# Down LoRA between token groups: expert weights transposed to the layout of the LoRA rows, in place of LoRA rows transposed to token order

## The reference

```python
gate = x @ W_gate + _lora(x, sA_gate, sB_gate, scale) + _expert_lora(x, A_gate, B_gate, w, scale)
up = x @ W_up + _lora(x, sA_up, sB_up, scale) + _expert_lora(x, A_up, B_up, w, scale)
hidden = jax.nn.silu(gate) * up
out = hidden @ W_down + _lora(hidden, sA_down, sB_down, scale) + _expert_lora(hidden, A_down, B_down, w, scale)
# _expert_lora: xA = einsum('bld,edr->bler', x, A); (einsum('bler,erd->bled', xA, Bm) * scale * w).sum(axis=2)
```

## Time and profile before

| | us |
|---|---|
| three executions | 732.37, 734.18, 735.18 |
| median | 734.18 |
| span of the profiled execution, first to last instruction | 731.8 |
| TensorE busy in it | 715.5 |
| VectorE busy | 376.6 |
| ScalarE busy | 262.3 |
| start of the attention's first denominators | 171.9 |
| first border between groups (last down projection to next first down) | 383.6 to 402.1 |
| last down projection's last matmul starts | 720.6 |

### The profile page before, as it was taken

How to read it: one execution, slowest core, us unless ns; L and a number is a source line. 1 busy time by engine, 2 the same in 40 slices (tenths; PEclk the granted TensorE clock), 3 DMA queues, 4 the chain that set the end, 5 groups by cost and what they waited for, 6 DMA issues and landing times.

```text
span 731.8 us, 10129 instructions
## 1 busy us (share of the span) xinstructions
PE 715.5 (98%) x3356; PEld 574.9 (79%) x3356; DVE 376.6 (51%) x715; ACT 262.3 (36%) x409; POOL 123.6 (17%) x293
## 2 busy tenths in 40 slices
PE   7999999998999999999999999999999999999997
PEld 5888888875776767888878888888788888788886
DVE  5666556676666665444425444325543335534433
ACT  4343333563431432333324333324333325333222
POOL 3544555420632641000000000000000000000000
PEclk9999999999999999999999999999999999999999
DMA  7766555326555645000010500010500001300001
GB/s 244 273 201 199 184 187 202 115 116 241 232 182 203 226 149 197 34 0 0 0 57 25 206 0 0 0 27 30 229 0 0 0 2 56 115 0 0 0 0 59
DMA packets 22754, 72.99 MB, mean 100 GB/s; under 512 B 2560, under 2 KB 2816, under 8 KB 20688
## 3 DMA queue, kind: packets, MB, share of 16 engines
q1 hardware_dynamic: 22560, 72.46, 27.8%
q0 software_dynamic: 176, 0.30, 0.2%
HBM read 51.78 MB, written 20.97 MB: 99 GB/s over the span
## 4 chain that ended last, share of the span: by engine, by line
PE 88%; DVE 5%; issue 2%; POOL 2%; ACT 1%; DMA 1%; DVEq 0%; SPq 0%; POOLq 0%
PE bank L1115 18%; PE bank L1116 18%; PE bank L1117 18%; PE bank L1326 17%; PE bank L1301 5%; PE bank L1313 4%; PE bank L1226 2%; PE bank L1142 1%; PE bank L1352 1%; PE bank L1178 1%; DMA w_raw<-in_wkT 1%; PE bank L1150 1%; PE bank L1132 1%; PE bank L1234 1%; PE bank L1345 1%
## 5 line engine op out<-in xcount | busy, mean ns | idle before, releaser
L1115 PE MATMUL bank<-x,up_h 128*128 (+1 forms) x352 | 138.1, 392 | 2.1 <-DVE qf L985 1.2
L1116 PE MATMUL bank<-x,up_h 128*128 (+1 forms) x352 | 137.3, 390 | 0.0
L1117 PE MATMUL bank<-x,up_l 128*128 (+1 forms) x352 | 137.0, 389 | 0.0
L1055 DVE TENSOR_TENSOR hf<-bank,silu 128x512 f32<-128x512 f32 x44 | 30.4, 691 | 157.2 <-issue 137.5
L1115 PEld LDWEIGHTS bank<-x,up_h 128*128 128x128 f32 x352 | 66.1, 188 | 19.0 <-issue 2.1
L594 ACT ACTIVATE hid_h<-hf 128x512 fp32r<-128x512 f32 x44 | 27.8, 632 | 146.3 <-DVE hf L1055 146.3
L1117 PEld LDWEIGHTS bank<-x,up_l 128*128 128x128 f32 x352 | 66.1, 188 | 14.1
L1116 PEld LDWEIGHTS bank<-x,up_h 128*128 128x128 f32 x352 | 66.1, 188 | 13.8
L799 DVE TENSOR_TENSOR up_l<-up_raw,up_h 128x1024 fp32r<-128x1024 f32 x45 | 55.6, 1236 | 37.1 <-ACT up_h L594 37.0
L1326 PE MATMUL bank<-dn_h,hid_h 128*128 128x512 f32 x176 | 69.8, 396 | 0.0
L1326 PE MATMUL bank<-dn_h,hid_l 128*128 128x512 f32 x176 | 69.2, 393 | 0.0
(11 more groups left out here) (169 smaller groups left out, 1260.3 us busy)
## 6 DMA issues: line engine op xcount, KB each, us to landing
x<-scr_x SPq DMA_DIRECT2D x8, 2048.0 KB, 7.6
up_raw<-in_ffn_up SPq DMA_DIRECT2D x11, 768.0 KB, 5.2
scr_x<-xt SPq DMA_DIRECT2D x16, 512.0 KB, 4.8
xin<-in_x SPq DMA_DIRECT2D x16, 256.0 KB, 5.8
scr_z<-zt SPq DMA_DIRECT2D x16, 256.0 KB, 2.2
x3r<-in_x SPq DMA_DIRECT2D x16, 256.0 KB, 3.5
scr_att<-x3r SPq DMA_DIRECT2D x16, 256.0 KB, 2.1
z<-scr_z SPq DMA_DIRECT2D x4, 1024.0 KB, 5.0
```

The source lines that it names most:

```text
L1055: nc.vector.tensor_tensor(hf[:], ps_u[:], silu[:], ALU.mult).then_inc(h_done, 1)
L1115: nc.tensor.matmul(dst, lh, rh, start=start, stop=False, **kw)
L1116: nc.tensor.matmul(dst, lh, rl, start=False, stop=False, **kw)
L1117: return nc.tensor.matmul(dst, ll, rh, start=False, stop=stop, **kw)
```

## The change

The rows of `ps_zd` are no longer turned. Instead the expert weights are: at the start of each group VectorE spreads `wtok` of the group to `wcur` (`weights_of`: each weight eight times, and 1/8 in the columns behind for the shared LoRA), TensorE transposes its four tiles into `ps_t` (`weights_transposed`, behind the second chunk's up projection), and ScalarE copies them to `wexp` (`weights_out`). At the end of the group one multiply on VectorE gives the weighted rows, `zw` = `ps_zd` x `wexp` (`lora_down_weighted`). ScalarE rounds them twice (`zd1`, `zd2`), VectorE subtracts for the low parts (`lora_down_lo`), and the two tiles are used as the weights of `lora_add`, which moves one gate projection earlier, to just behind the up projection of the next group's first chunk. The shared columns of `A_down` are computed twice (80 rows in `ps_zd` instead of 72), since the low part of the shared rows is kept beside the high one. In the tail the transposes and the filler of 9 go; the filler of 6 stays. For `bdn`, VectorE's two subtractions become one over rows 0 to 95, and ScalarE rounds the eight shared rows once more and signals `bdn_done`, behind `queries(0, (2, 3))`.

```diff
@@ -42,7 +42,8 @@
...
 UPC = UPW + UPB
-DNC = D + ER + R
+DNR = ER + 2 * R
+DNC = D + DNR
 SH = ER
...
@@ -200,11 +201,11 @@
...
         res = at("res", [P, GT, D])
-        zdc = at("zdc", [ER + R, GN])
-        zdf = at("zdf", [P, GT, ER])
-        zds = at("zds", [P, GT, R])
-        zdst = at("zdst", [P, GT, 2, P], F32R)
-        zdt = at("zdt", [P, 2, GT, P], F32R)
+        wcur = at("wcur", [P, GT, P])
+        wexp = at("wexp", [P, GN])
+        zw = at("zw", [P, GN])
+        zd1 = at("zd1", [P, GN], F32R)
+        zd2 = at("zd2", [P, GN], F32R)
...
@@ -712,6 +713,8 @@
...
             queries(0, (2, 3))
+            act.wait_ge(bdnl_done, 1)
+            round_to(bdn[SH:SH + R, 1], bdn_raw[SH:SH + R, 1]).then_inc(bdn_done, 1)
             lora_out(TILES - 1)
...
@@ -736,6 +739,8 @@
...
                     split_up(c + 1, 1 - s, n)
+                if before is not None:
+                    lora_down_hi(before)
                 if not start:
...
@@ -744,36 +749,25 @@
...
                     split_dn(c, s, 0)
-                if before is not None:
-                    stack_hi(before)
                 act.wait_ge(h_done, n + 2)
...
-            def lora_copy(g):
-
-                act.wait_ge(zd_ready, g + 1)
-                round_to(zdc[:], ps_zd[0:ER + R, :]).then_inc(zdc_done, 1)
-
-            def stack_hi(g):
-                act.wait_ge(zdf_done, g + 1)
-                round_to(zdst[:, :, :, 0:ER], zdf[:].unsqueeze(2).to_broadcast([P, GT, 2, ER]))
-                round_to(shared_cols(zdst), zds[:].unsqueeze(2).to_broadcast([P, GT, 2, R])).then_inc(zdh_done, 1)
-
-            def stack_out(g):
-                act.wait_ge(zdt_ready, g + 1)
-                round_to(zdt[:, 0].rearrange("p k n -> p (k n)"), ps_t[:])
-                round_to(zdt[:, 1].rearrange("p k n -> p (k n)"), ps_zd[:]).then_inc(zdt_done, 1)
+            def lora_down_hi(g):
+                act.wait_ge(zw_done, g + 1)
+                round_to(zd1[0:ER, :], zw[0:ER, :])
+                round_to(zd2[0:DNR, :], zw[0:DNR, :]).then_inc(zdh_done, 1)
+
+            def weights_out(g):
+                act.wait_ge(wexp_ready, g + 1)
+                round_to(wexp[:], ps_t[:]).then_inc(wexp_done, 1)
...
                 n = g * FC
-                if before is not None:
-                    lora_copy(before)
                 chunk(n, 0, 0, first=True, before=before)
-                if before is not None:
-                    stack_out(before)
                 chunk(n + 1, 1, 1)
+                weights_out(g)
                 with act.Fori(0, (FC - 3) // 2) as i:
...
@@ -787,9 +781,7 @@
...
                 group(g, before=g - 1)
-            lora_copy(GROUPS - 1)
-            stack_hi(GROUPS - 1)
-            stack_out(GROUPS - 1)
+            lora_down_hi(GROUPS - 1)
...
@@ -1012,9 +1004,7 @@
...
             dve.wait_ge(bdnh_done, 1)
-            for r0, r1 in ((0, ER), (SH2, P)):
-                last = sub(bdn[r0:r1, 1], bdn_raw[r0:r1, 1], bdn[r0:r1, 1])
-            last.then_inc(bdn_done, 1)
+            sub(bdn[0:SH2, 1], bdn_raw[0:SH2, 1], bdn[0:SH2, 1]).then_inc(bdnl_done, 1)
             queries(0, (2, 3))
...
@@ -1059,18 +1049,20 @@
...
-            def lora_rows(g):
-
-                dve.wait_ge(zdr_ready, g + 1)
-                zd = ps_t[:, 0:GT * (ER + R)].rearrange("p (j n) -> p j n", j=GT)
-                nc.vector.tensor_scalar(zds[:], zd[:, :, ER:], RSCALE, None, ALU.mult)
-                nc.vector.tensor_tensor(zdf[:].rearrange("p j (e r) -> p j e r", e=E),
-                                        zd[:, :, 0:ER].rearrange("p j (e r) -> p j e r", e=E),
-                                        wtok[:, bass.ds(g * GT, GT), :].unsqueeze(3).to_broadcast([P, GT, E, R]),
-                                        ALU.mult).then_inc(zdf_done, 1)
-                dve.wait_ge(zdf_done, g + 1)
+            def weights_of(g):
+                nc.vector.tensor_copy(wcur[:, :, 0:ER].rearrange("p j (e r) -> p j e r", e=E),
+                                      wtok[:, bass.ds(g * GT, GT), :].unsqueeze(3).to_broadcast([P, GT, E, R])
+                                      ).then_inc(wcur_done, 1)
+
+            def lora_down_weighted(g):
+                dve.wait_ge(zd_ready, g + 1)
+                dve.wait_ge(wexp_done, g + 1)
+                nc.vector.tensor_tensor(zw[0:DNR, :], ps_zd[0:DNR, :], wexp[0:DNR, :], ALU.mult).then_inc(zw_done, 1)
+
+            def lora_down_lo(g):
                 dve.wait_ge(zdh_done, g + 1)
-                stack_lo(zdst, zdf, zds).then_inc(zdst_done, 1)
+                sub(zd1[ER:2 * ER, :], zw[0:ER, :], zd1[0:ER, :])
+                sub(zd2[SH2:SH2 + R, :], zw[SH:SH + R, :], zd2[SH:SH + R, :]).then_inc(zdl_done, 1)
...
@@ -1081,12 +1073,16 @@
...
                 n = g * FC
-                chunk(n, 0, 0, due=None if before is None else lambda: lora_rows(before))
+                if before is not None:
+                    lora_down_weighted(before)
+                chunk(n, 0, 0, due=None if before is None else lambda: lora_down_lo(before))
                 if before is None:
...
                     dve.wait_ge(att_out, 16 * TILES)
-                    nc.vector.memset(zdst[:].bitcast(F32), 0.0).then_inc(late_clear, 1)
+                    nc.vector.memset(wcur[:, :, ER:], RSCALE)
+                    nc.vector.memset(zd2[:].bitcast(F32), 0.0).then_inc(late_clear, 1)
                     dve.wait_ge(late_clear, 1)
+                weights_of(g)
                 chunk(n + 1, 1, 1, due=None if before is None else lambda: results(before))
...
@@ -1103,7 +1099,8 @@
...
                 late_group(g, before=g - 1)
-            lora_rows(GROUPS - 1)
+            lora_down_weighted(GROUPS - 1)
+            lora_down_lo(GROUPS - 1)
             results(GROUPS - 1)
...
@@ -1310,7 +1307,7 @@
...
                     for i, (h, w) in enumerate(((hid_h, dn_h), (hid_h, dn_l), (hid_l, dn_h))):
-                        d = nc.tensor.matmul(ps_zd[0:ER + R, :], w[:, s, D:], h[:, s, :], start=(first and i == 0),
+                        d = nc.tensor.matmul(ps_zd[0:DNR, :], w[:, s, D:], h[:, s, :], start=(first and i == 0),
                                              stop=(last and i == 2), skip_group_check=True)
...
@@ -1329,29 +1326,20 @@
...
-            def lora_rows(g):
-
-                pe.wait_ge(zdc_done, g + 1)
+            def weights_transposed(g):
+                pe.wait_ge(wcur_done, g + 1)
                 for j in range(GT):
-                    last = nc.tensor.transpose(ps_t[:, j * (ER + R):(j + 1) * (ER + R)], zdc[:, j * P:(j + 1) * P],
-                                               ident[0:ER + R, 0:ER + R])
-                last.then_inc(zdr_ready, 1)
-
-            def lora_stack(g):
-
-                pe.wait_ge(zdst_done, g + 1)
-                for b, dst in enumerate((ps_t, ps_zd)):
-                    for j in range(GT):
-                        last = nc.tensor.transpose(dst[:, j * P:(j + 1) * P], zdst[:, j, b, :].bitcast(F32), ident[:])
-                last.then_inc(zdt_ready, 1)
+                    last = nc.tensor.transpose(ps_t[:, j * P:(j + 1) * P], wcur[:, j, :], ident[:])
+                last.then_inc(wexp_ready, 1)
             def lora_add(g):
-                pe.wait_ge(zdt_done, g + 1)
+                pe.wait_ge(zdl_done, g + 1)
                 for j in range(GT):
-                    for b in range(2):
-                        last = nc.tensor.matmul(ps_out[j][:], zdt[:, b, j, :], bdn[:, b, :], start=False, stop=(b == 1),
-                                                skip_group_check=True)
-                    last.then_inc(o_ready, 1)
+                    cols = slice(j * P, (j + 1) * P)
+                    nc.tensor.matmul(ps_out[j][:], zd1[:, cols], bdn[:, 0, :], start=False, stop=False,
+                                     skip_group_check=True)
+                    nc.tensor.matmul(ps_out[j][:], zd2[:, cols], bdn[:, 1, :], start=False, stop=True,
+                                     skip_group_check=True).then_inc(o_ready, 1)
...
@@ -1364,14 +1352,11 @@
...
                     gate_or_up(g, n, 0, 0, first=True)
-                    lora_rows(before)
                     gate_or_up(g, n, 0, 1)
-                if before is not None:
-                    lora_stack(before)
+                    lora_add(before)
                 gate_or_up(g, n + 1, 1, 0)
-                if before is not None:
-                    lora_add(before)
                 gate_or_up(g, n + 1, 1, 1)
+                weights_transposed(g)
                 down(g, n, 0, first=True)
...
@@ -1386,9 +1371,6 @@
...
                 group(g, before=g - 1)
-            lora_rows(GROUPS - 1)
-            keep_busy(ps_g, 9)
-            lora_stack(GROUPS - 1)
             keep_busy(ps_g, 6)
...
@@ -1432,7 +1414,7 @@
...
         ffn_up[:, :, UPW + a * 2 * P:UPW + (a + 1) * 2 * P] = b
-    ffn_dn = np.concatenate([given["W_down"], experts_in(given["A_down"]), given["sA_down"]], axis=1)
```

(13 more changed lines are left out.)

## The result

The changed kernel takes 723.92 us (median of four executions, 723.72 to 724.70) against 734.02 for the kernel before (four executions too), a ratio of 0.987 with a 95% interval of 0.9854 to 0.9887. That is 10.1 us less. Forecast were 727.9 us and a range of 725.1 to 730.9: the direction is right, the gain is larger than the range allowed, by 1.2 us at its lower end.

A forecast was written before the change was run, and what follows sets the result against it. TensorE was taken to bound the kernel (busy 715.5 of 731.8 us). Terms -0.69 (`bdn`) - 3.54 + 1.96 (transposes) - 0.60 (`res`) - 3.41 (tail) = -6.28 us, from 734.18 to 727.9; range 725.1 to 730.9.

The forecast's parts named there:

- The borders: Three borders between token groups: removed transposes save 3.54 us in all; new weight transposes cost 0.49 us a group.
- The transposes of group 0: Four new transposes of expert weights in the first group, which has no border saving: 0.49 us added.
- The wait on `res`: First down projection after each border waits 0.2 us for VectorE's adds; claimed to go, saving 0.60 us.
- The new waits: At borders `lora_add` waits for `zdl_done`; claimed slack 3.4 us, so no cost.
- Rival C: Slower: border `lora_add` waits for late `zdl_done`, three times, up to 17.1 us, time 745; chance 0.02, plus 0.02 for something between.
- The tail: After the last down matmul: transposes and filler go, `lora_add` starts at 722.3 instead of 725.71, saving 3.41 us.
- within 1.6 us of the last down matmul: Tail: sign that the forecast is right, `lora_add` following the last down matmul this closely.
- `bdn`: Start of attention: one VectorE subtraction instead of two, so the last `qf` and all behind start 0.69 us earlier.
- rival A: Start of attention: the shorter TensorE gap may keep the clock up, another 1.68 us gone, 726.2 us; chance 0.3.
- cost nothing more: LoRA matmuls with output grown from 72 to 80 rows stay 512 columns wide, so no added cost.
- 1% of a rounding off the path: Wider `dn_raw` (592 against 584 columns) adds 1% to a 0.69 us rounding off the path.
- the 2.4 that were carried over: Difference between the kernel before's median (734.18) and its profiled span (731.8), added to the forecast span.

The follow-up runs named there:

- two subtractions: Changed kernel with VectorE's one `bdn` subtraction cut into two again (rows 0 to 63, 64 to 95); 726.55 us, ratio 0.9893.
- 80 columns: Kernel before with `ffn_dn` rows of 592 columns and 80 LoRA weight columns used; first to last down projection 426.27 us against 427.42.
- the shifted tiles: Kernel before with a dummy tile moving all tiles behind `dn_raw` by 352 bytes; first to last down projection 427.40 us against 427.42.
- 600 columns: Kernel before with `ffn_dn` rows padded to 600 columns, 72 LoRA columns used; first to last down projection 426.69 us against 427.42.
- 592 columns: Kernel before with `ffn_dn` rows padded from 584 to 592 columns, 72 LoRA columns used; first to last down projection 426.66 us against 427.42.

## Why the prediction was wrong

**The borders: right.** Forecast 1.18 saved in transposes, 0.20 of the wait and 0.49 added, 0.89 us a border. Measured 1.02; 0.06 of the 0.13 more are the added transposes, which took 0.43, and the rest has no run of its own. The transposes of group 0, 0.49, measured 0.43. The slot (0.11 us), not the duration (0.27), was the right price, as the run with doubled transposes shows.

**The wait on `res`: gone, for a reason that I had only half.** I had named the earlier `lora_add` and ScalarE's missing copies together. The run with `lora_add` put back shows that its place gives nothing; the run with it moved forward shows that it can do harm, through `hf`. Of what is left (the copies, the up projection 0.30 us earlier without the `zdc` transposes, and 0.43 us of transposes in front of the down projection) no run separates the parts.

**The new waits: right.** `zdl_done` was placed 3.4 us early at the border; it is 3.25 us early (386.67 to 389.92). In the earliest place the wait on it was 0.1 us at most. Rival C had no ground. The point from which a reordering does harm lay elsewhere, in the queue behind `hf`.

**The tail: right.** Forecast 3.41, measured 3.38; the filler and the chain through `zw` end within 0.2 us of each other, as worked out (last filler matmul from 715.59, VectorE's subtractions until 715.79, `lora_add` at 715.85). The sign of "within 1.6 us of the last down matmul" holds from the end of its slot (1.48), not from its start (1.71).

**`bdn`: right, a little small.** Forecast 0.69, measured 0.82. From the start of the first subtraction to the next `qf` step it was 1.42 us (167.47 to 168.89) and is 0.61 (167.23 to 167.84), not 0.73 as placed; the kernel with two subtractions gives the same 0.8. `kcur` at 169.86 was early enough.

**The clock: rival A, given 0.3, took place.** The `kcur` matmuls took 3.59 us instead of 5.29, 1.70 us, its price within 0.02. Is the shorter gap the cause? Fourteen profiles exist by now. With a gap of 2.4 us the clock fell at this place in four of six (before, 80 columns, the shifted tiles, 600 columns; not with 592 columns and not with two subtractions). With 1.0 to 1.6 us it fell in none of eight. That speaks for the gap, but it rests on profiles of several kernels, and the run with the gap put back did not decide it: its clock fell in the first stage. No profile has the fall at both places, and five of the ten without it here have it in the first stage, so a fall there may be what kept this place free. Without those five it is four of five with the long gap and none of four with the short one. So the shorter gap as the cause is likely and not shown, and the 1.70 us are a gain in a part of the executions. The Trainium skill (TensorE: Matmul & The Clock Gate, Why this matters for your kernels) warns of idle gaps between bursts of matmuls. The profiles agree with the direction and show that the same gap does not always lead to a fall.

**The step that failed** is the one that had the LoRA's matmuls "cost nothing more" with 80 rows instead of 72, since a slot was 0.23 us "whatever their number of weight columns", and that saw in the wider `dn_raw` only 1% of a rounding off the path. Both were looked at for a cost alone, and no gain was put beside it. The wider rows give 0.76 us and the eight columns 0.39, of which 1.08 lie inside the groups. Rival A alone, 726.2, would have stayed inside the range; with this term it is 727.9 - 1.70 - 1.08 = 725.1, the lower end itself.

In spans the account closes. Forecast was about 725.5 and measured 721.9, 3.6 us less: 1.70 for the clock, 1.08 inside the groups, 0.13 for `bdn`, 3 x 0.13 for the borders, 0.06 for the transposes of group 0 and 0.24 by which the two profiles differ ahead of the change. The forecast of the median has a part of chance as well. Every execution on record takes between 1.75 and 1.96 us more than its span, so the 2.4 that were carried over held some 0.6 by which the middle execution of the kernel before was slower than the profiled one. All nine executions of the changed kernel have their median at 724.5, still below the range. The range's lower end had the clock's gain and 1.1 us for scatter, and no room for a second gain on the same side.

## What to carry to other kernels

Where one engine has no gaps, price an edit by the distance between starts, and give every operand whose shape or pitch changes a bound for a gain as well as for a cost: 25 ns in each of 44 chunks is as much as a border between groups. Turning a small table of weights early in a group, instead of the data on the path at its end, took a serial tail from 5.1 to 1.7 us; but a step moved forward on the busy engine pushes what another engine's queue waits for. Compare kernels that differ by less than the clock's scatter by landmarks in their timelines, not by their medians: the stretch from the first down projection to the last is 423.36 us in both profiles of the changed kernel and in the three of its variants with another order for `bdn` or with `lora_add` put back, while their spans differ by 2.8 us.

## What was not expected of the hardware

- The width of the rows of `dn_h` and `dn_l` shows in TensorE's pace, though the matmuls read the same columns: 2368 and 2400 bytes against 2336 took 0.76 and 0.73 us off 427.4 us, while a shift of all tiles by 352 bytes changed 0.02.
- A matmul with 80 columns of weights instead of 72, with the same 512 moving columns, made the stretch 0.39 us shorter over 132 such matmuls, not longer (one profile of each; the changed kernel's pace inside its groups is the same as with 80 columns).
- The granted clock of TensorE falls at a place or not from one execution to the next: behind the same gap of 2.4 us in four profiles of six, and in five profiles of fourteen in the first stage, somewhere between 10.5 and 15.3 us.
